# Image tokens' values, output weights and part of the query stack moved in the setup of a two-branch attention kernel

## The reference

```python
q = split_heads(x @ w_q)
out_text = sdpa(q, text @ w_k, text @ w_v)
mask_ip = ip_mask(bbox)                     # 0 or -10000, by place and box
out_ip = sdpa(q, ip_h @ w_k_ip, ip_h @ w_v_ip, mask=mask_ip)
out = (merge_heads(out_text) + merge_heads(out_ip)) @ w_out + b_out + x
```

## Time and profile before

| | |
|---|---|
| median of 3 runs | 704.74 us (704.57 to 705.28) |
| the profiled execution | 703.88 us, span 702.1 us |
| mean granted clock of TensorE | 0.998 of full speed |
| busy: PE, DVE, ACT, POOL | 684.2, 534.3, 290.7, 215.6 us |
| DMA | 89.42 MB, mean 127 GB/s |

### The profile page before, as it was taken

How to read it: one execution, slowest core, us unless ns; L and a number is a source line. 1 busy time by engine, 2 the same in 40 slices (tenths; PEclk the granted TensorE clock), 3 DMA queues, 4 the chain that set the end, 5 groups by cost and what they waited for, 6 DMA issues and landing times.

```text
span 702.1 us, 19355 instructions
## 1 busy us (share of the span) xinstructions
PE 684.2 (97%) x6625; PEld 635.2 (90%) x6625; DVE 534.3 (76%) x1690; ACT 290.7 (41%) x636; POOL 215.6 (31%) x371
## 2 busy tenths in 40 slices
PE   9997999999999999999999999999999999999996
PEld 8787778999899999999998989999999989899876
DVE  4434569797978788887979787878888797878784
ACT  1222363442517272634435161726354352617161
POOL 5321006050424233151504242332415041423333
PEclk9999999999999999999999999999999999999999
DMA  9989434444435262635444352626353443435221
GB/s 297 379 245 206 138 80 108 138 97 133 108 88 149 71 179 70 157 86 137 98 132 105 89 147 76 176 67 162 90 133 97 129 104 103 128 82 131 68 76 39
DMA packets 52513, 89.42 MB, mean 127 GB/s; under 512 B 9440, under 2 KB 23520, under 8 KB 52460
## 3 DMA queue, kind: packets, MB, share of 16 engines
q1 hardware_dynamic: 51024, 86.09, 45.6%
q10 hardware_dynamic: 1068, 1.66, 0.9%
q0 software_dynamic: 384, 1.18, 0.7%
HBM read 39.21 MB, written 10.62 MB: 71 GB/s over the span
## 4 chain that ended last, share of the span: by engine, by line
PE 85%; SPq 5%; DVE 4%; DMA 2%; issue 2%; ACTq 0%; ACT 0%; POOL 0%; DVEq 0%; POOLq 0%
PE psum L1100 38%; PE psum L1162 9%; PE psum L1212 9%; PE psum L1196 6%; PE psum L1191 5%; SPq L418 4%; PE psum L1220 3%; PE psum L1030 3%; PE psum L1221 2%; PE psum L1235 2%; PE psum L967 2%; PE psum L1060 1%; PE psum L1218 1%; DMA k_stack<-k_lo 1%; PE psum L943 1%
## 5 line engine op out<-in xcount | busy, mean ns | idle before, releaser
L574 POOL TENSOR_TENSOR attn<-o_parts 128x128 f32<-128x128 f32 x160 | 73.3, 458 | 414.7 <-DVE o_parts L906 385.3
L865 DVE TENSOR_REDUCE neg_max<-psum 128x2 f32<-128x292 f32 x320 | 144.7, 452 | 49.3 <-PE psum L1162 49.0
L1100 PE MATMUL psum<-wo_both,at_hi 128*128 128x320 f32 x640 | 153.3, 313 | 0.0
L1162 PE MATMUL psum<-k_stack,q_stack 104*128 104x154 f32 x640 | 112.6, 286 | 4.1 <-DVE neg_max L866 1.9
L1100 PE MATMUL psum<-xt_hi,wq_hi 128*128 128x256 f32 x400 | 114.1, 285 | 1.2 <-DVE q_lo L857 1.2
L1100 PE MATMUL psum<-xt_lo,wq_hi 128*128 128x256 f32 x400 | 111.2, 278 | 0.0
L1100 PE MATMUL psum<-xt_hi,wq_lo 128*128 128x256 f32 x400 | 111.0, 278 | 0.0
L893 DVE TENSOR_TENSOR p_lo<-psum,p_hi 128x512 f16<-128x512 f32 x160 | 107.8, 682 | 2.6 <-ACT psum L718 2.5
L1100 PEld LDWEIGHTS psum<-wo_both,at_hi 128*128 128x128 f32 x640 | 109.7, 188 | 0.0
L716 ACT ACTIVATE p_hi<-psum 128x512 f16<-128x512 f32 x160 | 95.2, 595 | 28.6 <-PE psum L1191 28.5
L1212 PE MATMUL psum<-v_tail,p_tail 128*128 128x264 f32 x320 | 101.5, 398 | 2.0 <-ACT p_tail L720 0.9
(11 more groups left out here) (99 smaller groups left out, 1274.5 us busy)
## 6 DMA issues: line engine op xcount, KB each, us to landing
q_stack<-q_hi SPq DMA_DIRECT2D x128, 96.0 KB
x_in<-in_x SPq DMA_DIRECT2D x16, 640.0 KB, 5.3
x_res<-in_x SPq DMA_DIRECT2D x16, 640.0 KB, 5.3
out<-out_sb SPq DMA_DIRECT2D x32, 320.0 KB
q_stack<-q_hi SPq DMA_DIRECT2D x128, 64.0 KB
q_stack<-q_lo SPq DMA_DIRECT2D x60, 96.0 KB
q_stack<-q_lo SPq DMA_DIRECT2D x60, 64.0 KB
q_stack<-aux_a SPq DMA_DIRECT2D x48, 64.0 KB, 2.4
```

What stands on the lines that cost most here:

```text
L574: nc.gpsimd.tensor_tensor(cols, o_parts[:, qt, 0:4, :], o_parts[:, qt, 4:8, :], ALU.add).then_inc(att_half, 1)
L865: nc.vector.tensor_reduce(dst[:, :, 0], src[:, :, 0:TEXT], AX_X, ALU.max, negate=True)
L1100: last = nc.tensor.matmul(ps, l(c), r(c), start=(i == 0), stop=(i == len(terms) - 1))
L1162: last = nc.tensor.matmul(scores[sc % 2][:, i * CTX:(i + 1) * CTX], q_stack[0:ROW_MAX, query_slot(h), P * qt:P * (qt + 1)], k_stack[batch] ...
```

## The change

- The units' order becomes main, main, image, image, text, text, main, main. Before the first scores stands one main unit; the second is spread over set A's scores. The first image unit stands ahead of `AUX` 0 in step 1, the second ahead of the third score step of set B, both text units ahead of the fifth, both last main units ahead of the sixth. Banks, copies and splits follow.
- SP issues `w_v_ip` behind the first stack and mask, ahead of the second and third piece of the text value weights (it was ahead of the second block's x_in).
- SP issues `w_out` in step 1 behind the rows of `AUX` 0, once four units are done (it was at the end of step 0, once two were). Its split moves: ScalarE's five casts from ahead of query product 1 to ahead of product 2 of step 1, VectorE's five subtractions to behind products 2 (two) and 3 (three).
- GpSimd issues the third part (high, rows 64 to 95) of set A's first stack, on a semaphore of its own, after its first keys and once three query products are out; SP issues only the first.

```diff
--- before.py
+++ after.py
@@ -152,21 +152,20 @@
 V_CUT = 256
-V_UNITS = [("ip", 0), ("ip", 1), ("main", 0, 0, V_CUT), ("main", 1, 0, V_CUT),
+V_UNITS = [("main", 0, 0, V_CUT), ("main", 1, 0, V_CUT), ("ip", 0), ("ip", 1),
            ("text", 0), ("text", 1), ("main", 0, V_CUT, D), ("main", 1, V_CUT, D)]
 V_MAIN = [n for n, unit in enumerate(V_UNITS) if unit[0] == "main"]
-V_BANKS = (5, 6, 7, 5, 6, 6, 5, 7)
+V_BANKS = (7, 5, 6, 6, 6, 7, 5, 6)
 V_PLACES = {
-    (0, "S", 0, 0, 0): ((0, 0, 8), (1, 0, 8)), (0, "S", 0, 1, 0): ((2, 0, 2),), (0, "S", 1, 0, 0): ((2, 2, 4),),
-    (0, "S", 1, 0, 1): ((2, 4, 6),), (0, "S", 1, 1, 0): ((2, 6, 8),), (0, "S", 1, 1, 1): ((3, 0, 2),),
-    (0, "S", 2, 0, 0): ((3, 2, 4),), (0, "S", 2, 1, 0): ((3, 4, 6),),
-    (1, "AUX", 0): ((3, 6, 8), (4, 0, 8)), (1, "S", 3, 1, 0): ((5, 0, 8),), (1, "S", 4, 0, 0): ((6, 0, 8),),
-    (1, "S", 4, 0, 1): ((7, 0, 8),),
+    (0, "S", 0, 0, 0): ((0, 0, 8),), (0, "S", 0, 1, 0): ((1, 0, 2),), (0, "S", 1, 0, 0): ((1, 2, 4),),
+    (0, "S", 1, 0, 1): ((1, 4, 6),), (0, "S", 1, 1, 0): ((1, 6, 8),),
+    (1, "AUX", 0): ((2, 0, 8),), (1, "S", 3, 1, 0): ((3, 0, 8),), (1, "S", 4, 0, 0): ((4, 0, 8), (5, 0, 8)),
+    (1, "S", 4, 0, 1): ((6, 0, 8), (7, 0, 8)),
 }
-V_COPY_PLACES = {(0, "S", 0, 0, 0): (0, 1), (0, "S", 2, 0, 0): (2,), (1, "Q", 0): (3, 4), (1, "Q", 1): (5,), (1, "ST", 0, 2): (6, 7)}
-V_SPLIT_PLACES = {(1, "S", 3, 0, 0): (2, 3), (1, "S", 4, 0, 1): (6, 7)}
-W_O_HIGH = {("Q", 1): (0, 1, 2, 3, 4)}
-W_O_LOW = {("S", 3, 1, 1): (0, 1, 2), ("S", 4, 0, 0): (3, 4)}
+V_COPY_PLACES = {(0, "S", 1, 0, 0): (0,), (0, "S", 2, 0, 0): (1,), (1, "Q", 0): (2,), (1, "Q", 1): (3,), (1, "ST", 0, 2): (4, 5, 6, 7)}
+V_SPLIT_PLACES = {(1, "S", 3, 0, 0): (0, 1), (1, "S", 4, 0, 1): (6, 7)}
+W_O_HIGH = {("Q", 2): (0, 1, 2, 3, 4)}
+W_O_LOW = {("Q", 2): (0, 1), ("Q", 3): (2, 3, 4)}
 GENERAL = {"X": 1, "Q": 1, "AUX": 1, "PV": 1, "O": 1}
@@ -363,6 +362,7 @@
         x_freed, q_freed, aux_freed = sem("x_bank_freed"), sem("q_bank_freed"), sem("aux_bank_freed")
         q_ready, qh_done = sem("q_product"), sem("q_hi_ready")
         stack_in = [sem("stack_a_in"), sem("stack_b_in")]
+        stack_own = sem("first_stack_a_in_by_gpsimd")
         s_ready, s_freed = sem("scores_ready"), sem("maxima_taken")
         split_hi, split_done = sem("max_hi_ready"), [sem("max_a_split"), sem("max_b_split")]
         aux_ready, aux_in = sem("maxima_transposed"), [sem(f"aux_in{g}") for g in range(GROUPS)]
@@ -408,7 +408,11 @@
             engine.wait_ge(s_kst[b], 16 * 4 * (2 - b))
             engine.wait_ge(s_kst_own[b], 16 * 4 * (1 + b))
-        def queries_to_stack(queue, n, parts):
+        def stack_count(n, blocks):
+
+            return blocks * (16 * N_STACK_DMAS) - (16 * 4 if n == 0 else 0)
+
+        def queries_to_stack(queue, n, parts, landed=None):
             g0, g1 = (SET_A, SET_B)[n][0], (SET_A, SET_B)[n][-1] + 1
             for row, part in parts:
@@ -416,7 +420,7 @@
                 for j in range(4):
                     first = 4 * g0 + (g1 - g0) * j
                     queue.dma_start(q_stack[row:row + DH, first:first + g1 - g0, :].bitcast(F32),
-                                    src[DH * j:DH * (j + 1), g0:g1, :].bitcast(F32)).then_inc(stack_in[n], 16)
+                                    src[DH * j:DH * (j + 1), g0:g1, :].bitcast(F32)).then_inc(landed or stack_in[n], 16)
         block = stack.enter_context(nc.Block())
@@ -439,9 +443,6 @@
             load_values(0)
-            sp.wait_ge(s_kip, 1)
-            sp.dma_start(w_v_ip, wv_ip.rearrange("(c p) n -> p c n", p=P)).then_inc(s_wv_ip, 16)
-
             sp.wait_ge(xt_ready, NX)
             sp.dma_start(x_in[:], x_rows[QB:2 * QB, :].rearrange("(a p) d -> p a d", p=P)).then_inc(x_loaded, 16)
@@ -465,6 +466,10 @@
                             src = aux_rows[n][16 * i:16 * (i + 1), :].bitcast(F32).unsqueeze(1).to_broadcast([16, 4, QB])
                             sp.dma_start(q_stack[ROW_MAX:STACK, query_slots(g), :].bitcast(F32), src
                                          ).then_inc(aux_in[g], 16)
+                        if second and n == 0:
+
+                            sp.wait_ge(s_vp, 4)
+                            sp.dma_start(wo_raw[:, KC:2 * KC, :], wo.rearrange("(c p) n -> p c n", p=P)).then_inc(s_wo, 16)
                         if second and n == 1:
                             sp.wait_ge(s_vp, len(V_UNITS))
@@ -488,11 +493,14 @@
                         if it.back:
                             sp.wait_ge(st_ready, t * ST_ALL - ST_ALL + 1 + max(ST_TURN[(g, u)] for g in groups for u in range(3)))
-                        queries_to_stack(sp, n, STACK_PARTS if it.back else STACK_PARTS[::2])
+                        queries_to_stack(sp, n, STACK_PARTS if it.back else STACK_PARTS[:1] if n == 0 else STACK_PARTS[::2])
                         src = mask_dram[:, bass.ds(t * QB, QB)].unsqueeze(1).to_broadcast([IP, 4 * len(groups), QB])
                         sp.dma_start(q_stack[ROW_MASK:ROW_MAX, 4 * g0:4 * g1, :].bitcast(F32), src
                                      ).then_inc(stack_in[n], 16)
                         if not it.back and n == 0:
+
+                            sp.wait_ge(s_kip, 1)
+                            sp.dma_start(w_v_ip, wv_ip.rearrange("(c p) n -> p c n", p=P)).then_inc(s_wv_ip, 16)
                             load_values(1)
                             load_values(2)
                     if kind == "STORE":
@@ -505,9 +513,6 @@
                         sp.dma_start(out_rows[bass.ds(t * QB - QB - P, P), :], out_sb[:, 1, :]).then_inc(stored, 16)
                 if not it.back:
                     keys_to_stack(sp, 1, K_PARTS[2:], s_kst[1])
-
-                    sp.wait_ge(s_vp, 2)
-                    sp.dma_start(wo_raw[:, KC:2 * KC, :], wo.rearrange("(c p) n -> p c n", p=P)).then_inc(s_wo, 16)
             iterations(sp, body)
@@ -548,6 +553,8 @@
             pool.wait_ge(s_klo, GROUPS)
             pool.wait_ge(s_klo_ip, 1)
             keys_to_stack(nc.gpsimd, 0, K_PARTS[1:2], s_kst_own[0])
+            pool.wait_ge(q_freed, 3)
+            queries_to_stack(nc.gpsimd, 0, STACK_PARTS[2:], stack_own)
             pool.wait_ge(q_freed, GROUPS)
             keys_to_stack(nc.gpsimd, 1, K_PARTS[:2], s_kst_own[1])
             for b in range(BATCHES):
@@ -699,7 +706,9 @@
                         act.wait_ge(q_ready, t * GROUPS + g + 1)
                         if it.back:
-                            act.wait_ge(stack_in[n], t * (16 * N_STACK_DMAS))
+                            act.wait_ge(stack_in[n], stack_count(n, t))
+                            if isinstance(t, int) and t == 1 and n == 0:
+                                act.wait_ge(stack_own, 16 * 4)
                         nc.scalar.activation(q_hi[:, g, :], bank_a[:, 0:QB], ACT.Copy).then_inc(qh_done, 1)
                         if not it.back and g in (3, 4):
@@ -1037,11 +1046,11 @@
                     keys, b, *cols = V_UNITS[n]
                     if (n, first) == (0, 0):
-                        pe.wait_ge(s_wv_ip, 16)
+                        pe.wait_ge(s_wv[0], 16)
                         pe.wait_ge(s_klo, GROUPS)
                     if (n, first) == (2, 0):
-                        pe.wait_ge(s_wv[0], 16)
+                        pe.wait_ge(s_wv_ip, 16)
                     if (n, first) == (4, 0):
                         pe.wait_ge(s_wv[1], 16)
@@ -1153,7 +1162,9 @@
                             n = 0 if g in SET_A else 1
                             blocks = t + 1 if stage == FRONT else t + 0
-                            pe.wait_ge(stack_in[n], blocks * (16 * N_STACK_DMAS))
+                            pe.wait_ge(stack_in[n], stack_count(n, blocks))
+                            if not it.back and n == 0:
+                                pe.wait_ge(stack_own, 16 * 4)
                         if it.back or sc >= 2:
                             pe.wait_ge(s_freed, it.sc0 + sc - 1)
@@ -1200,7 +1211,7 @@
                         g, qt = args
                         if isinstance(t, int) and t == 1 and (g, qt) == (0, 0):
-                            pe.wait_ge(s_vc, 5)
+                            pe.wait_ge(s_vc, 7)
                             pe.wait_ge(s_vsplit, 3 * V_PARTS)
                         if qt == 0:
```

## The result

| | before | after |
|---|---|---|
| median of the runs taken together | 705.01 us (704.57 to 706.05) | 720.32 us (719.32 to 721.84) |
| ratio to before | | 1.0214, 95% interval 1.0175 to 1.0253 |
| profiled execution, span | 703.88 us, 702.1 us | 721.84 us, 720.0 us |
| granted clock of TensorE, mean | 0.998 | 0.981 |

The account below looks back on a forecast made before the run. DMA was taken to bound the setup from 55 to 72 us, with TensorE full in the steady blocks; 0.3 + 4.5 + 4.0 + 1.7 = 10.5 us on 704.74 us gave 715.2 us, range 708.0 to 720.0 us.

Parts of the forecast that it names:

- my three signs of being wrong: Set B's scores before 69 us; DMA share well under 1 from 55 to 70 us; TensorE's third-group PV wait no longer.
- When the second stack lands: Setup, start of set B's scores: stack in at 72.0 us against 71.68, +0.3 us, bounds -2.0 and +3.3.
- Two small units behind the wait: Behind set B's wait: second image unit and first text unit, two times 2.3 us, nothing covering them, +4.5 us.
- The split of w_out: First softmax, step 1: later casts and subtractions delay the normalising TensorE waits for by 4.0 us, lower bound 1.2.
- The clock: TensorE behind the 9 us wait: one spell of lowered clock in dense work, +1.7 us, bounds 0 and 3.4.
- The first scores: Setup: with one main unit ahead, first scores start at 52.4 us, 2.9 us earlier than 55.28 us.
- GpSimd's part: Set A's first stack: last part might land at 54 to 55 us, covered by the 9 us wait; worth nothing.
- Starved twice: Rival: second stack at 75 us and two spells at half clock, 719.9 us; chance 0.09.
- The output weights hide: Rival: TensorE's lag leaves ScalarE time, the w_out split costs 1.2 instead of 4.0 us, 712.4 us; chance 0.14.
- The image weights flow in the slack: Faster rival: DMA room before 55 us takes the load, set B's scores start at 63 us, 701.7 us; chance 0.09.

Follow-up runs that it names:

- e10: Changed kernel with both text pieces issued behind the second stack and last keys, image weights still between the stacks; 715.73 us, ratio 1.0164.
- e1: Changed kernel with the image value weights loaded early again, as in the kernel before; 715.18 us, ratio 1.0132.
- e8: Changed kernel with early image weights, early w_out split, and the last two text pieces issued behind the last keys; 702.35 us, ratio 0.9966.
- e9: e8 without GpSimd's part of the first stack, its four DMAs back on SP; 705.18 us, ratio 0.9997.
- e2: Kernel before with only the later split of w_out; 708.72 us, ratio 1.0038.
- e7: Changed kernel with only the split of w_out put back early, around query product 1 of step 1; 717.12 us, ratio 1.0169.
- e6: Changed kernel with the image value weights loaded early and the split of w_out early again; 710.17 us, ratio 1.0067.
- e4: Changed kernel with more filler products: 54 instead of 16 before the first scores, 44 before set B's; 720.08 us, ratio 1.0200.
- e8b: The same kernel as e8, run once more beside e9; 703.01 us, ratio 0.9970.
- e11: Changed kernel with SP issuing the image weights behind both stacks and the last keys, ahead of the text pieces; 718.39 us, ratio 1.0184.
- e5: Changed kernel with GpSimd instead of SP issuing the image value weights, behind its keys of batch 1; 720.67 us, ratio 1.0235.
- e3: Kernel before with only GpSimd's part of set A's first stack added; 707.34 us, ratio 1.0022.

## Why the prediction was right and wrong

**The sign and the mechanism** were right: a long wait before set B's scores, small units behind it, a dearer split, a slower clock. Two of my three signs of being wrong did not come: set B's scores start after 69 us, and the share is 1.03 or more from 55 to 70 us. The third did, with the split. Term by term:

**When the second stack lands: the step that failed.** I took +0.3 us, between 69.7 and 75.0. It was 76.84, +5.2, beyond the late bound. The step was the sum of DMA work, 32.5 engine-us with the weights, at a share of 1.09. It counts work and assumes that the engines are fed until it is done. They were fed with the wrong things first: SP issues no faster than its queue takes what went before, and it stood for 14.91 us in the text pieces, so the stack's DMAs began at 63.74 us, took 8.61 us to issue, and landed while the share was 0.73 and then 0.28. The rows showed the sign of this: the earlier trace rows have the second stack's eight DMAs issued over 10.58 us where the first took 5.00. I said that they were held and went on to sum engine time. e10 bounds the size: with the image weights still there and only the text pieces out of the way, set B's scores start at 72.17 us, my 72.0, and the median is 4.6 us below the changed kernel, 10.55 us above before, my 10.5. That the same numbers meet is in part luck: e10's stack is no longer what TensorE waits for, the image weights are, and its 10.0 us of span divide otherwise than I had them (0.5, 5.9, 3.9 and -0.3 us by the four marks).

**Two small units behind the wait**, forecast +4.5: measured 3.9 us wherever the clock stays up (e1, e8 and e9: 24.6 to 24.7 us against 20.76). The units last as forecast (2.38 us the first). The other 0.6 us is a wait that goes. Before, TensorE stood between two score steps of set B for VectorE's maxima:

```profile
77.30 0.45 PE L1162 MATMUL psum<-k_stack,q_stack 104*128 104x154 f32 x2 [0.49 <-DVE neg_max L866]
```

In e1, e8 and the changed kernel no such wait stands in this stretch. I had taken it to be in both. The two units are the one price that no place of the load removes.

**The split of w_out**, forecast +4.0: +3.9 in the trace of the changed kernel, +3.5 in e2, -3.2 and -5.0 in the medians of e7 and e6. The size and the end of the path hold, what TensorE does on the way was wrong. ScalarE and VectorE were as forecast:

```profile
109.07 3.25 ACT L619 ACTIVATE wo_both<-wo_raw 128x640 fp32r<-128x640 f32 x5
112.19 0.40 ACT L712 ACTIVATE q_hi<-psum 128x256 fp32r<-128x256 f32 x1
112.46 0.41 ACT L729 ACTIVATE p_tail<-psum 128x256 f32<-128x256 f32 x1
```

```profile
112.62 0.42 DVE L866 TENSOR_TENSOR q_lo<-psum,q_hi 128x256 fp32r<-128x256 f32 x1 [2.72 <-ACT q_hi L712]
112.96 1.55 DVE L796 TENSOR_TENSOR wo_both<-wo_raw,wo_both 128x640 fp32r<-128x640 f32 x2
```

2.72 us of VectorE's idling against the 2.8 forecast. But TensorE pays first for the exp of the tail behind `q_hi`, 2.25 us, and then for the clock: from 113.8 to 117.2 us it is granted 0.50.

```profile
113.80:117.20 3.40, 3.40 (x27) 3.40 (x25) 3.33 (x10) 2.04 (x5) 1.49 (x4) 0.50 0.98 291
```

That is 1.7 us; the wait of the third group, to which I had given all of the 4.0, is shorter than before:

```profile
121.47 0.71 PE L1223 MATMUL psum<-v_tail,p_tail 128*128 128x264 f32 x2 [0.44 <-DVE o_parts L918]
```

By my own sign I was wrong here: this wait is no longer than before. But it still ends last. This value product starts 17.0 us behind the first transposed scores instead of 13.1, 3.9 us later; what TensorE loses ahead of it is only taken out of this wait. e2 bears that out: there the clock stays at 1.00 behind the 2.25 us wait, this wait is 1.14 us, and the product still comes 3.5 us later. So of the 1.7 us of clock at most some 0.4 us is added to the time.

**The clock**, forecast +1.7 with 3.4 as upper bound: too small. In 20 us stretches, one less the granted clock times 20 gives 2.2 + 3.2 + 1.6 + 1.8 us from 40 to 120 us (none before) and 5.2 us near the end (before 1.8). The 5.4 us before 80 us fall partly in waits and cost less than they count. On the later path the clock costs 3.0 us behind set B's scores (e4's difference), 1.7 behind the first transposed scores, within the 3.9 of the split, and the +2.0 of the steady part. So outside the split it is near 5 us of span, of which the lower clock near the end belongs to the profiled run in part. Over the runs the same shows: before has a median clock of 0.995 (the 23 runs beside e8b to e11), the changed kernel 0.985 (4 runs), and among those 23 the span falls by 4.3 us for each 0.01 of clock; at that slope, an estimate, some 4.5 of the 15.3 us.

**The first scores**, forecast at 52.4 us: 57.66. TensorE was ready at 53.0 and waited for ScalarE's low part. I had priced GpSimd's part at "54 to 55 us" and left ScalarE's out. The issues of ScalarE and of SP in the changed kernel are

```profile
46.13 3.46 ACTq L422 DMA_DIRECT2D q_stack<-q_lo  x4
47.94 0.80 SPq L503 DMA_DIRECT2D wo_raw<-in_L_xattn_w_v_ip  x1
```

and in e5, whose first scores start at 53.70 us,

```profile
46.29 3.22 ACTq L422 DMA_DIRECT2D q_stack<-q_lo  x4
49.09 1.47 SPq L442 DMA_DIRECT2D w_kv<-in_L_xattn_w_v  x2
```

In the changed kernel SP's load goes out 1.65 us before ScalarE is through with its four, in e5 0.42 us. In all six runs in which the first scores come at 56.7 us or later (the changed kernel, e1, e3, e4, e6, e7) this lead is 1.57 to 2.13 us; in e5 and e10 it is 0.4 us, and they come at 53.70 and 54.21 us though a large load is under way. So a load of SP's that gets in ahead of ScalarE's small DMAs is what goes with the late stack, and GpSimd's part, which makes SP sooner ready, lets it in (e3); why SP is 0.9 us later there in e10 than in the changed kernel, with the same instructions up to that load, is not known. It did cost nothing at the end, as I argued: e3 and the later wait cover it.

**The rivals.** "Starved twice" (719.9 us) was nearest, by its stack at 75 us and its two spells. "The output weights hide" fell with the marks of e2 (+3.5 us) and with e6 and e7. "The image weights flow in the slack" fell; but what it named as deciding, set B's scores at 63 us, comes about in e8 (64.73 us; 702.35 us against its 701.7), once the text pieces are put last, the image weights load early and the split stands early too. The rule of the Trainium skill on several issuers (Trainium Kernel Development and Optimization, Key Constraints) is that they save only issue time, and I took that to be worth nothing for GpSimd's part. e3 agrees (no change). e9 shows when it is worth something: there SP's issue time itself ends last, the mask going out at 49.89 instead of 48.06 us, and the part is worth 2.2 us. By the Trainium skill's rule that the throttled state of the clock is the default (TensorE: Matmul & The Clock Gate, What's actually happening) a fall had to come in waits as long as these; the trace agrees (0.58, 0.63).

**Left open:** why the clock near the end differs between profiled executions (1.8 us before, 5.2 in the changed kernel, 1.8 in e4, 7.0 in e11), with the same work there; a version of e8 with the old unit order, which was not tried; and what fills SP's queue. The two text pieces move in smaller packets than the image weights (from 52 to 54 us 494 of 497 packets are under 2 KB in e1, 8 of 226 in the changed kernel), so the number of packets may decide rather than the bytes; no run separates them.

## What to carry to other kernels

Sum the DMA work to see whether a transfer can be in time, then walk each issuing queue in order and ask what the issuing engine stands in. The text pieces, issued while the 2560 KB load of the same queue was under way, held SP for 14.91, 6.79 and 4.91 us (1.3 to 2.4 us without it), and everything behind them went out late; eight small DMAs right behind one large load were not held (e10). The order by first use is what counts: here the loads needed last (the text pieces) had to go behind the two small stacks, and the one load that is 2.6 MB had to stay early, where it is hidden. Price a wait of TensorE of a few microseconds with its clock behind it, 1.6 to 3 us for each here, less what a later wait covers, and put late setup work where the engines idle, not at the start of a softmax.

## What the runs showed of the hardware that I had not expected

**How long issuing takes depends on what the queue holds.** The same two text pieces (1.5 MB) took SP 1.40 us before, 14.91 us in the changed kernel, 6.79 us in e10 and 1.33 us in e8; the second stack's eight DMAs 10.58, 8.61, 5.01 and 7.20 us. They take longest right behind the text pieces (8.16 to 12.64 us, e7 and e5), not right behind the larger image weights (5.01 us, e10).

**How long 2560 KB take** varies with what else is under way: 16.4 us issued at 23 us, 19.9 us behind the first stack, 22.1 us issued by GpSimd, 9.7 us behind both stacks with the text pieces following (e11). At 378 GB/s, the best stretch of before, it would be 6.9 us.

**A fall of the clock behind a short wait comes or doesn't.** The 2.60 us gap of before left it at 1.00; in e2 a gap of 2.20 us at the same place was followed by 0.61:

```profile
68.00:72.00 4.00, 3.98 (x67) 3.33 (x67) 0.00 (x0) 0.24 (x1) 0.00 (x0) 0.61 1.06 158
```

and the text unit in it took 3.69 us instead of 2.38. A wait of 1.48 us (e9) was enough for 0.64. The same 2.25 us wait for `p_tail` is followed by 0.50 in the changed kernel and by 1.00 in e2 (100 to 104 us). The 23 runs of the kernel before beside e8b to e11 spread from 702.2 to 709.9 us, roughly along their clock (1.000 to 0.988), and with 12 runs against them an interval is still 0.23% to either side.
